# State space of a two-layer kernel: B and C rows by DMA instead of by matmul, the products with B on GpSimd, one scan over both channel halves

## The reference

```
for n in range(16):                     # each state, over all 512 tokens t
    h[c, t] = exp(-A[c, n] * dt[c, t]) * h[c, t - 1] + B[n, t] * dt[c, t] * xc[c, t]
    y[c, t] += C[n, t] * h[c, t]
y = (y + D * xc) * silu(z)
```

## Time and profile before

| | |
|---|---|
| median of 3 runs | 5074.1 us (5063.56 to 5074.44) |
| profiled execution: time, span | 5073.88 us, 5071.8 us |
| busy: PE, DVE, ACT, POOL | 3776.8, 2788.1, 1820.8, 1456.7 us |
| the stage that changes, projection of the first batch to the last tail step | about 3300 to 4842 us of the span |

### The profile page before, as it was taken

One profiled execution on the slowest core, in us unless ns is written; L12 is line 12 of the kernel. 1 busy time (PEld: TensorE's weight loads), 2 busy tenths in 40 slices (PEclk: granted clock), 3 DMA queues, 4 the chain that ended last, 5 costly groups with the idle time before them and its releaser, 6 DMA issues.

```text
span 5071.8 us, 134037 instructions
## 1 busy us (share of the span) xinstructions
PE 3776.8 (74%) x60154; PEld 2898.2 (57%) x60154; DVE 2788.1 (55%) x4939; ACT 1820.8 (36%) x2940; POOL 1456.7 (29%) x1396
## 2 busy tenths in 40 slices
PE   6888888888888888889899991166666666666342
PEld 4777777787777778778788881123323333333121
DVE  5354453545445354543355553477958769778812
ACT  2333233333423333332466661034342443343311
POOL 2221313222131322213444435222313213223322
PEclk7999998999999999999899996577776777777566
DMA  5340000000000000000544441000000000000011
GB/s 191 120 138 24 24 23 22 21 11 20 16 16 15 13 14 9 18 7 14 186 155 154 155 135 36 13 1 1 1 1 1 1 1 1 1 1 1 0 69 52
DMA packets 165196, 212.96 MB, mean 42 GB/s; under 512 B 82120, under 2 KB 143952, under 8 KB 158224
## 3 DMA queue, kind: packets, MB, share of 16 engines
q0 software_dynamic: 22992, 107.78, 6.4%
q1 hardware_dynamic: 98160, 43.65, 3.2%
q10 hardware_dynamic: 43472, 52.96, 3.1%
HBM read 146.43 MB, written 69.97 MB: 43 GB/s over the span
## 4 chain that ended last, share of the span: by engine, by line
PE 19%; issue 17%; DVE 7%; POOL 6%; ACT 2%; DMA 1%; SPq 0%; another core or an unknown queue 0%; POOLq 0%; DVEq 0%; ACTq 0%
PE psum L1787 5%; PE psum L1794 3%; POOL ss_y L2750 2%; PE psum L1814 1%; PE psum L1800 1%; PE psum L1778 1%; POOL e_h L1971 1%; DVE at_mx L2445 1%; PE psum L2320 1%; PE psum L3143 1%; PE psum L2323 1%; ACT at_pt L2394 1%; POOL routed L3216 1%; POOL hg L3226 1%; DVE ss_h L2719 1%
## 5 line engine op out<-in xcount | busy, mean ns | idle before, releaser
L2750 POOL TENSOR_TENSOR ss_y<-ss_y,ss_h 128x512 f32<-128x512 f32 x256 | 319.4, 1269 | 921.1 <-DVE ss_h L2719 921.1
L873 DVE TENSOR_TENSOR sd_z<-psum,sd_z 128x512 f32<-128x512 f32 x320 | 219.1, 689 | 406.4 <-PE psum L741 406.4
L2713 DVE TENSOR_TENSOR_SCAN ss_h<-ss_da,ss_h 128x512 f32<-128x512 f32 x256 | 330.2, 1330 | 10.6 <-ACT ss_da L2633 9.5
L920 POOL TENSOR_TENSOR sd_z<-id,s_up 128x512 f32<-128x512 f32 x64 | 81.4, 1272 | 841.2 <-DVE s_up L879 840.6
L1787 PE MATMUL psum<-e_h,e_mid_w 128*128 128x256 f32 x1248 | 284.1, 381 | 1.0 <-DMA e_mid_w<-table_mid,r_table_i 1.0
L1787 PEld LDWEIGHTS psum<-e_h,e_mid_w 128*128 128x128 f32 x1248 | 238.4, 191 | 34.4 <-issue 1.7
L1182 POOL TENSOR_TENSOR out_sq<-st_h 128x512 f32<-128x512 f32 x64 | 66.6, 1041 | 649.8 <-PE psum L1114 387.9
L741 PE MATMUL psum<-s_low,s_up 64*64 64x64 f32 x6144 | 226.4, 226 | 27.6 <-DVE sd_z L873 22.3
L741 PE MATMUL psum<-sd_z,s_do 64*64 64x64 f32 x6144 | 221.7, 226 | 26.7 <-ACT s_do L822 26.1
L741 PEld LDWEIGHTS psum<-sd_z,s_do 64*64 64x64 f32 x6144 | 204.0, 141 | 60.0 <-issue 31.6
L2394 ACT ACTIVATE at_pt<-psum 128x512 f32<-128x512 f32 x320 | 165.2, 602 | 193.6 <-PE psum L2323 193.3
(11 more groups left out here) (477 smaller groups left out, 9996.4 us busy)
## 6 DMA issues: line engine op xcount, KB each, us to landing
answered<-ce_zeros ACTq DMA_DIRECT2D x19, 1024.0 KB, 5.2
routed<-ce_zeros ACTq DMA_DIRECT2D x16, 1024.0 KB, 9.2
st_eg<-gate_scratch SPq DMA_DIRECT2D x128, 128.0 KB, 5.3
table_mid<-in_t_mid ACTq DMA_DIRECT2D x4, 1536.0 KB, 8.0
m_w<-in_m_w SPq DMA_DIRECT2D x2, 2048.0 KB
table_down<-in_t_down ACTq DMA_DIRECT2D x1, 2560.0 KB, 12.1
g_x<-in_x SPq DMA_DIRECT2D x8, 256.0 KB, 6.0
xn_scratch<-g_xn_tok SPq DMA_DIRECT2D x8, 256.0 KB, 5.5
```

Of the source, the lines that this page charges most:

```text
L873: dve.tensor_tensor(d.z[:, :, :], bank[:, :].rearrange("p (a t) -> p a t", a=NP), d.z[:, :, :], ALU.add).then_inc(T.dve.give(r, name), 1)
L2713: dve.tensor_tensor_scan(h, Z.da[(2 * n + m) % 4][:, :], h, 0.0, ALU.mult, ALU.add).then_inc(sig(f"s{n}_{m}"), 1)
L2750: pool.tensor_tensor(Z.y[:, m, :], Z.y[:, m, :], Z.h[(2 * n + m) % 4][:, :], ALU.add).then_inc(Z.pool.give(b, f"y{n}_{m}"), 1)
```

## The change

B and C are no longer split and no longer spread by PE. ACT copies them once (32x512), SP stores them in a DRAM scratch (L2561 of the new file), and for each state SP loads the row pair, spread over 128 partitions (512 KB in SBUF), into one of three buffers `ss_rows` (L2569). The product with B moves from DVE to POOL, 128x1024 at once, two states ahead (L2743). The scan runs once over both halves (L2714; the first column of the second half of `ss_da` is held at zero). The product with C reads `ss_rows` instead of PSUM, 128x1024 at once (L2719). y is added in one 128x1024 instruction (L2762). The softplus chain works on both halves at once, written into `ss_dtx`. A state-space batch is now written in 40 steps (units), and in the turns of attention weights it takes two of them (`units`, L2233).

```
 class Stage1:
+        self.units = 1
+def units(line, go):
+    while True:
+        for _ in range(go.units):
+            if next(line, "end") == "end":
+                return
+        yield
             for turn, (kind, n) in enumerate(attention_turns(i)):
+                go.units = 2 if kind == "weights" else 1
 class StateSpace:
+    N_ROWS, N_H = 3, 3
-        self.bc3 = sb("ss_bc3", [6 * DS, S], BF16)
-        self.da = [sb(f"ss_da{i}", [P, S]) for i in range(4)]
-        self.h = [sb(f"ss_h{i}", [P, S]) for i in range(4)]
+        self.da = [sb(f"ss_da{i}", [P, DB, S]) for i in range(2)]
+        self.h = [sb(f"ss_h{i}", [P, DB, S]) for i in range(self.N_H)]
+        self.rows = [sb(f"ss_rows{i}", [P, 2, S]) for i in range(self.N_ROWS)]
+def state_space_sp(C, Z, bc_dram):
+        sp.wait_ge(*Z.act.at(b, "bc"))
+        sp.dma_start(bc_dram[b].rearrange("k n s -> (k n) s"), Z.bc[:, :]).then_inc(*Z.stored.up())
+        sp.wait_ge(*Z.stored.now())
+        for n in range(DS):
+            if b * DS + n >= Z.N_ROWS:
+                sp.wait_ge(*Z.pool.at(old_b, f"d{old_n}"))
+                sp.wait_ge(*Z.dve.at(old_b, f"m{old_n}"))
+            sp.dma_start(rows[:, :, :], bc_dram[b, :, n, :].partition_broadcast(P)).then_inc(sem, 16)
 def state_space_pe(C, A, Z, go):
-        def row(r, name):
-            pe.matmul((b5, b6)[r // DS][:, :], w["pick3"][:, r:r + 1].to_broadcast([6 * DS, P]), Z.bc3[:, :],
 def state_space_dve(C, A, Z, go):
-                dve.tensor_tensor(Z.h[(2 * n + m) % 4][:, :], b5[:, :], Z.dtx[:, m, :], ALU.mult)
-                dve.tensor_tensor_scan(h, Z.da[(2 * n + m) % 4][:, :], h, 0.0, ALU.mult, ALU.add)
-                dve.tensor_tensor(h, b6[:, :], h, ALU.mult)
+            dve.tensor_tensor_scan(flat, flat2(Z.da[n % 2][:, :, :]), flat, 0.0, ALU.mult, ALU.add)
+            dve.tensor_tensor(h[:, :, :], rows[:, 1, :].unsqueeze(1).to_broadcast([P, DB, S]), h[:, :, :], ALU.mult)
 def state_space_pool(C, A, Z, T, go):
+        def drive(n):
+            pool.wait_ge(*loaded)
+                pool.wait_ge(*Z.pool.at(b, f"y{n - Z.N_H}_all"))
+            pool.tensor_tensor(Z.h_of(b, n)[:, :, :], rows[:, 0, :].unsqueeze(1).to_broadcast([P, DB, S]), Z.dtx[:, :, :], ALU.mult)
-                pool.tensor_tensor(Z.y[:, m, :], Z.y[:, m, :], Z.h[(2 * n + m) % 4][:, :], ALU.add)
+            if n + 2 < DS:
+                drive(n + 2)
+            pool.wait_ge(*Z.dve.at(b, f"m{n}"))
+            pool.tensor_tensor(Z.y[:, :, :], Z.y[:, :, :], Z.h_of(b, n)[:, :, :], ALU.add)
```

More of the change, by code:

```diff
@@ L173, in constants @@
                        pattern=[[HD, NH1]], channel_multiplier=-1).then_inc(wave(), 1)
[L174 to L177, removed]
     return made
@@ L2495, in attention_pool @@
                 slots_of(t + 1)
-            for _ in attention_turns(i):
+            for kind, _ in attention_turns(i):
+                go.units = 2 if kind == "weights" else 1
                 yield
@@ L2526, in __init__ @@
+        self.h = [sb(f"ss_h{i}", [P, DB, S]) for i in range(self.N_H)]
+        self.rows = [sb(f"ss_rows{i}", [P, 2, S]) for i in range(self.N_ROWS)]
         self.y = sb("ss_y", [P, DB, S])
         self.zeroed = C.loads("ss_zeroed")
-        self.pe = C.steps("ss_matmuls", ["x0", "x1", "z0", "z1", "di", "bc", "dt0", "dt1"] + sum([[f"B{n}", f"C{n}"] for n in range(DS)], []))
-        self.act = C.steps("ss_activations", ["raw0", "silu0", "raw1", "silu1", "sz0", "sz1", "di", "bc", "dt0", "e0", "l0", "dt1", "e1", "l1"]
+        self.stored = C.loads("ss_bc_stored")
@@ L2530, in __init__ @@
+        self.rows_in = [C.loads(f"ss_rows_in{i}") for i in range(self.N_ROWS)]
+        self.pe = C.steps("ss_matmuls", ["x0", "x1", "z0", "z1", "di", "bc", "dt0", "dt1"])
+        self.act = C.steps("ss_activations", ["raw0", "raw1", "silu0", "silu1", "sz0", "sz1", "di", "bc", "dt0", "dt1", "e", "l"]
                            + sum([[f"a{n}_0", f"a{n}_1"] for n in range(DS)], []))
[L2531 to L2534, removed]
@@ L2535, in __init__, with h_of @@
-        self.pool = C.steps("ss_sums", ["y0", "y1"] + sum([[f"y{n}_0", f"y{n}_1"] for n in range(DS)], []))
+        self.dve = C.steps("ss_vectors", self.CONV + ["abs", "dt", "dtx"] + sum([[f"s{n}", f"m{n}"] for n in range(DS)], []) + ["f"])
+        self.pool = C.steps("ss_sums", ["y0", "y1", "d0", "d1"]
+                            + sum([([f"d{n + 2}"] if n + 2 < DS else []) + [f"y{n}_all"] for n in range(DS)], []))
+    def h_of(self, b, n):
+        return self.h[(b * DS + n) % self.N_H]
@@ L2723, in state_space_dve @@
-        for m in range(DB):
-            dve.wait_ge(*Z.pool.at(b, f"y{DS - 1}_{m}"))
-            dve.tensor_tensor(Z.y[:, m, :], Z.y[:, m, :], Z.sz[:, m, :], ALU.mult).then_inc(sig(f"f{m}"), 1)
-        go.scanned = b
+            dve.wait_ge(*Z.pool.at(b - 1, f"d{DS - 1}"))
+        dve.scalar_tensor_tensor(out=Z.dtx[:, :, :], in0=Z.dt[:, :, :], scalar=-1.0, in1=Z.dt[:, :, :], op0=ALU.mult, op1=ALU.min).then_inc(sig("abs"), 1)
+        yield
+        dve.wait_ge(*Z.act.at(b, "l"))
+        dve.scalar_tensor_tensor(out=Z.dt[:, :, :], in0=Z.dt[:, :, :], scalar=0.0, in1=Z.dtx[:, :, :], op0=ALU.max, op1=ALU.add).then_inc(sig("dt"), 1)
@@ new lines, in state_space_dve @@
+        dve.wait_ge(*was("dt"))
+        dve.tensor_tensor(Z.dtx[:, :, :], Z.dt[:, :, :], Z.xc[:, :, :], ALU.mult).then_inc(sig("dtx"), 1)
+        yield
+        yield
+        for n in range(DS):
+            h = Z.h_of(b, n)
+            dve.wait_ge(*Z.act.at(b, f"a{n}_1"))
+            dve.wait_ge(*Z.pool.at(b, f"d{n}"))
+            flat = flat2(h[:, :, :])
+            dve.tensor_tensor_scan(flat, flat2(Z.da[n % 2][:, :, :]), flat, 0.0, ALU.mult, ALU.add).then_inc(sig(f"s{n}"), 1)
+            yield
+            rows, loaded = Z.rows_of(b, n)
+            dve.wait_ge(*loaded)
+            dve.wait_ge(*was(f"s{n}"))
+            dve.tensor_tensor(h[:, :, :], rows[:, 1, :].unsqueeze(1).to_broadcast([P, DB, S]), h[:, :, :], ALU.mult).then_inc(sig(f"m{n}"), 1)
+            yield
@@ L2736, in state_space_pool @@
             yield
-        for _ in range(2 * DB + 2 + DB):
+        def drive(n):
+            rows, loaded = Z.rows_of(b, n)
+            pool.wait_ge(*loaded)
+            if n >= Z.N_H:
+                pool.wait_ge(*Z.pool.at(b, f"y{n - Z.N_H}_all"))
+            elif b:
+                pool.wait_ge(*Z.pool.at(b - 1, f"y{DS - Z.N_H + n}_all"))
+            pool.tensor_tensor(Z.h_of(b, n)[:, :, :], rows[:, 0, :].unsqueeze(1).to_broadcast([P, DB, S]), Z.dtx[:, :, :],
+                               ALU.mult).then_inc(Z.pool.give(b, f"d{n}"), 1)
+        for _ in range(6):
             yield
@@ L2743, in state_space_pool @@
             pool.tensor_scalar(Z.y[:, m, :], Z.xc[:, m, :], w["d_param"][:, m:m + 1], None, ALU.mult).then_inc(Z.pool.give(b, f"y{m}"), 1)
+        pool.wait_ge(*Z.dve.at(b, "dtx"))
+        drive(0)
+        drive(1)
         yield
```

167 lines of the change are left out of this document (64 added, 103 removed).

## The result

The changed kernel takes **5106.45 us**, median of 4 runs (5102.16 to 5112.56), against 5071.27 for the kernel before in the same series (5063.56 to 5074.44). The ratio is 1.0073, 95% interval 1.0055 to 1.009: slower by 35 us by the medians and 37 by the ratio, more than the 0.2% that a measurement can tell. The profiled execution took 5104.52 us, span 5102.7.

What follows compares the result with a forecast made beforehand. DVE bounds the windows with scans (93% busy), engine-to-engine chains those between. Stage: 42 + 980 + 120 + 434 + 36 = 1612 us against 1542, +70, so 5145 us; this case's range 5085 to 5200, overall 4990 to 5230.

Steps and rivals of the forecast that it cites:

- What goes from DVE: State space on DVE: the drives (products with B) leave, 1.2 us per state, about 155 us over 128 states.
- What GpSimd gets: Per state a drive and a 1024-column addition, 2.35 us each (bounds 2.09 and 2.54), 4.7 us instead of 2.5.
- What it costs: A state's four instructions can't run side by side: 8.26 us less 0.6 overlap, 7.65 instead of 5.4.
- The batch of 140 us: Windows with scans: 140 us per batch, where before the mean is 122; the last batch 120 instead of 85.
- Between the scans: Seven windows between two batches' scans: 62 us each instead of 68, the only gain of the shorter rotation.
- the bare turns: Rival: windows between grow to 72 us, ends and projections having no scans to hide behind; 5215 us, chance 0.08.
- The loads at nothing: Loads of a state's rows, 6 to 12 us to landing, priced at nothing because work on two states covers them.
- what would show it: Closing list of signs in profile and timeline for the forecast being right or wrong, such as scan medians and GpSimd's busy time.
- a median scan well over 2.4 us: Sign of being right, for 128x1024 scans on DVE; medians near 2.35 with DVE idle little would mean wrong.
- GpSimd waiting for `ss_rows`: Sign of being wrong: DVE or GpSimd waiting for the row buffers that the loads fill.
- The hidden standstill: Rival: GpSimd's work falls where DVE idles anyway or into reductions and short selection steps; about 4980 us, chance 0.31.

Runs made afterwards that it cites:

- e6_beside: Changed kernel with B and C out of PSUM again and each GpSimd addition waiting for the next state's scan; 4948.64 us, ratio 0.975 to the kernel before.

## Why the prediction was right, and where it was off

Forecast 5145, measured 5106, inside the range and on the forecast side. The mechanism holds; the size is too large by 39 us, and of the 71 us forecast about half came (35 to 37). That the sum came this near owes something to luck: the windows with scans were forecast 69 us too long and those between 35 too short.

**What goes from DVE.** 1.2 us per state went, and nothing of it was gained: on top of it came the standstill. Right.

**What GpSimd gets.** 2.35 us for 1024 columns; the shortest are 2.34 and 2.33 us. Right, and the lower bound of 2.09 was wrong.

**What it costs.** 7.65 us per state forecast, 7.58 measured where nothing else is on DVE; the four shortest durations add up to 8.15, so 0.6 us of overlap per state was the right reading of the earlier trace rows. The tiny addition confirms the cause. Selection's short steps wait as said: L3024, 128x15, up to 2.34 us.

**The batch of 140 us is the mis-sized term.** Measured: 131 us in the mean of the first seven (127 to 134), 114 instead of 120 in the last. The working was 12 states at 7.65 and 4 at 9.15, 128.4 us, to which I added 5 us for an expert's selection and 6.5 for the first drive and waits for PE. Two things in it don't belong to the window. The first drive (2.35 us) lies ahead of it: in batch 0 it starts at 3325.1, 8 us before the first scan at which the window begins. And the window ends with the last scan: in batch 0 it holds 16 scans and 15 products, so the last state counts with the 2.3 us of its scan and not with 7.65. These are 7.7 of the 9 us per batch. This is arithmetic on the trace; no run separates the rest, the 5 us for selection and the waits for PE. The number of reductions was no part of the error: the trace has 8 among the scans of batch 0 (before 9, not the 11 given ahead of the prediction).

**Between the scans** 62 us were forecast and 67 came (68 before), 35 us too few in sum, against the other error. The last product of a batch, 1.2 to 3.2 us, lies here and was not in the sum. The rest is the rival of the bare turns, at about half its size. The run with one step per turn, where attention runs ahead as before, has 60 us here, 8 less than before: that fits the gain expected from the merged softplus and the missing splitting, and the short rotation takes 7 of it back. Those 7 are 47 us in sum; one step per turn saves them and pays as much among the scans.

**The loads at nothing**: they land after 4.9 us, not 6 to 12, and cost 6 to 15 us. Their row in the waits view misleads: 148 us of waits are there, and nearly none of them in the time.

**Sign of a mistake in "what would show it"**: I asked for a median scan well over 2.4 us and named 2.35 as a sign against. It is 2.28, with a mean of 2.95. Most scans wait for nearly a whole GpSimd instruction (44 of 128 take over 3.6 us) or hardly at all (73 take under 2.4), so the median depends on who comes first (3.64 without loads) and says little. Nor does the excess of one kind: what stayed the same without loads is the excess over the shortest summed over all of DVE's instructions that wait (338 and 329 us). GpSimd waiting for `ss_rows` was also named as a sign against, and it came, 148 us, with the mechanism right.

**The hidden standstill**, my second case at 0.31, is ruled out by the tiny addition: GpSimd's addition alone costs 178 us, of the 300 that 128 of them take at 2.34. The other 122 cost no time, so part of GpSimd's work is hidden, but not enough.

How the parts add up, by the ratios, on 5074 us: new rotation, wide instructions and merged softplus with B and C still in PSUM, -55 us (0.9891); operands of drive and product out of SBUF by DMA instead, +65 (1.0019); drives to GpSimd, +27 (1.0073). A gain of 55 us lay under a loss of 92. No run takes the 55 apart.

## What to carry to other kernels

Before work is moved from DVE to GpSimd, count the inputs that DVE's remaining instructions have in SBUF: with two, the moved work is paid wherever DVE has nothing else to do beside it. Here the drives took 156 us (128 x 1.22) off DVE and put 299 (128 x 2.34) on GpSimd, and the time rose by 27, so some 180 of the 299 were paid (an estimate from these numbers). And an operand moved from PSUM to SBUF turns work that ran side by side into work in turn. Let GpSimd's instruction be released by a wait that makes it start under DVE's PSUM instructions, even if its data are ready earlier; here that took 71 us off a kernel with its operands in PSUM. It is not the placement alone that gave 4948.6 us, 2.5% below the kernel before: by the ratios the placement in the kernel before gives 13 us; with wide instructions and the merged softplus, at one step per turn, 31; and with two steps per turn 127. An order of work is therefore worth trying again once the alternation is gone. Read an engine's busy time as means against shortest durations, over all its instructions, since a fuller engine may be a blocked one.

## What was not expected of the hardware

- A GpSimd instruction of two columns is blocked as a large one is. In the run with the tiny addition it takes 188 ns at the shortest, and here, beside a scan that itself waited, 2.18 us:

```profile
4615.89 4.43 DVE L2714 TENSOR_TENSOR_SCAN ss_h<-ss_da,ss_h 128x1024 f32<-128x1024 f32 x1
4618.13 2.18 POOL L2762 TENSOR_TENSOR ss_y<-ss_y,ss_h 128x2 f32<-128x2 f32 x1
```

- DVE's `tensor_scalar` on 15 columns, with one tensor input, waits too (0.15 us alone, up to 2.34 in the changed kernel), while reductions out of PSUM do not (L2454 keeps its 2.28 us).
- One and the same move of steps in the rotation (one step per turn for two) costs 97 us in e6_beside and 9 us by the medians, nothing by the ratios, in the changed kernel: alternation can hide what an order is worth.
